# Layer 1's last row group normalised by GpSimd, and the query scales worked out in two parts

## The reference

```python
xn = _layernorm(x)                                 # (x - mean) / sqrt(var + 1e-5)
s = _L1_attn_ref(xn, L1_attn_W_qkv, L1_attn_W_out) # local attention in chunks of 64 rows, 16 heads of 8,
                                                   # plus a cross term with the mean keys of earlier chunks
# the gate, _L1_ffn_ref(xn, ...):
nx = xn * rsqrt(mean(xn * xn) + 1e-6) * g1         # _rmsnorm
Q = nx @ Wq.T ; Kc = nx @ Wkc.T ; Vc = nx @ Wvc.T  # 4 heads share keys and values, softmax over all rows
X = xn + attention(Q, Kc, Vc) @ Wo.T
g = silu(X + moe(_rmsnorm(X, g2)))
out = x + s * g
```

## Time and profile before

| what | value |
|---|---|
| time, median of 3 runs | 676.07 us (674.52 to 678.64) |
| the profiled execution's own time | 676.78 us |
| its span, first to last instruction | 674.6 us |
| granted TensorE clock, mean over the span | 0.966 |
| busy: PE / DVE / ACT / POOL | 609.1 / 484.8 / 353.0 / 356.0 us |
| the chunk stage's place in the span | about 212 to 305 us |

### The profile page before, as it was taken

One profiled execution on the slowest core, in us unless ns is written; L12 is line 12 of the kernel. 1 busy time (PEld: TensorE's weight loads), 2 busy tenths in 40 slices (PEclk: granted clock), 3 DMA queues, 4 the chain that ended last, 5 costly groups with the idle time before them and its releaser, 6 DMA issues.

```text
span 674.6 us, 12623 instructions
## 1 busy us (share of the span) xinstructions
PE 609.1 (90%) x4528; PEld 409.6 (61%) x4529; DVE 484.8 (72%) x1140; ACT 353.0 (52%) x714; POOL 356.0 (53%) x369
## 2 busy tenths in 40 slices
PE   4885889967998889896999999999999998999996
PEld 2564789944775556554555555555545553688885
DVE  5764345422987778769877788888888883788986
ACT  2643355421675445462667676777666666433231
POOL 6507400064463545170688887888787778524311
PEclk9989799988999899998999999999999998899999
DMA  9701012120000000000000000000000000000101
GB/s 290 321 1 48 31 48 63 47 55 24 1 0 2 1 2 3 2 3 1 0 1 1 1 0 2 1 1 1 0 1 1 1 0 1 1 1 1 32 1 32
DMA packets 16616, 17.33 MB, mean 26 GB/s; under 512 B 1712, under 2 KB 15024, under 8 KB 16176
## 3 DMA queue, kind: packets, MB, share of 16 engines
q1 hardware_dynamic: 15536, 14.49, 6.5%
q0 software_dynamic: 1024, 2.10, 1.0%
HBM read 11.34 MB, written 5.24 MB: 25 GB/s over the span
## 4 chain that ended last, share of the span: by engine, by line
PE 72%; DVE 14%; ACT 5%; issue 4%; another core or an unknown queue 2%; DMA 2%; POOL 1%; SPq 0%; DVEq 0%; ACTq 0%
PE ps L2052 13%; PE ps L2042 10%; PE ps L2032 8%; PE ps L2180 5%; PE ps L1764 4%; PE ps L1747 3%; DVE region L1086 3%; PE ps L1855 3%; PE ps L2170 2%; PE ps L2172 2%; PE ps L2171 2%; PE ps L1845 2%; DVE region L1067 1%; PE ps L1756 1%
## 5 line engine op out<-in xcount | busy, mean ns | idle before, releaser
L1086 DVE TENSOR_REDUCE region<-ps 128x1 f32<-128x512 f32 x256 | 160.7, 683 | 38.6 <-PE ps L2032 38.1
L1537 ACT ACTIVATE region<-ps 128x512 f32<-128x512 f32 x256 | 138.2, 600 | 60.3 <-PE ps L2042 60.3
L767 POOL TENSOR_TENSOR region<-region 128x512 f32<-128x512 f32 x80 | 109.0, 1365 | 42.5 <-ACT region L1537 38.5
L2042 PE MATMUL ps<-qmr,kr 98*128 98x512 f32 x256 | 111.8, 441 | 2.6 <-ACT region L1537 1.8
L2032 PE MATMUL ps<-kr,qmr 96*128 96x512 f32 x256 | 102.8, 411 | 2.1 <-DVE region L1086 1.3
L2052 PE MATMUL ps<-region 128*32 128x512 f32 x512 | 94.5, 616 | 0.0
L2059 PE MATMUL ps<-region,ones 128*32 128x512 f32 x192 | 94.3, 614 | 0.0
L772 POOL TENSOR_TENSOR region<-region 128x512 f32<-128x512 f32 x64 | 82.1, 1282 | 11.9 <-ACT region L1537 8.1
L2042 PEld LDWEIGHTS ps<-qmr,kr 98*128 98x128 f32 x256 | 48.7, 191 | 54.7 <-issue 28.9
L2032 PEld LDWEIGHTS ps<-kr,qmr 96*128 96x128 f32 x256 | 49.1, 193 | 15.6 <-DVE region L1086 9.0
L1764 PE MATMUL ps<-region 128*128 128x128 f32 x272 | 40.8, 298 | 19.1 <-ACT region L1384 12.9
(11 more groups left out here) (283 smaller groups left out, 1209.8 us busy)
## 6 DMA issues: line engine op xcount, KB each, us to landing
region<-in_w SPq DMA_DIRECT2D x2, 2048.0 KB, 12.9
slots_in<-zeros SPq DMA_DIRECT2D x1, 1536.0 KB, 9.4
region<-slots_in SPq DMA_DIRECT2D x6, 256.0 KB, 2.8
slots_out<-og SPq DMA_DIRECT2D x6, 256.0 KB, 2.4
e<-in_e SPq DMA_DIRECT2D x1, 1152.0 KB, 15.3
x<-in_x SPq DMA_DIRECT2D x4, 256.0 KB, 3.6
out<-y SPq DMA_DIRECT2D x3, 256.0 KB, 2.3
e<-in_e SPq DMA_DIRECT2D x1, 576.0 KB, 16.2
```

The lines of the kernel that those rows point to most:

```text
L767: ins = pool.tensor_tensor(o, held(tiles[0]), held(tiles[1]), ALU.add)
L1086: dve.tensor_reduce(mxp[:, u // HM, u % HM:u % HM + 1], bank(b), AX.X, ALU.max).then_inc(mx_read, 1)
L1537: act.activation(pm[:, t // 2, t % 2 * HM * P:(t % 2 + 1) * HM * P], bank(SCORE_BANKS[n % 3]), ACT.Exp, scale=SCM).then_inc(p_whole, 1)
L2042: pe.matmul(bank(SCORE_BANKS[n % 3]), kr[0:M_ROWS, t * P:(t + 1) * P], qr[0:M_ROWS, parity, :], start=True, stop=True).then_inc(st_filled, 1)
```

## The change

The four normalisations of row group 3 leave ScalarE's queue, where they stood between tile 2's exponentials and the first `qkv` drain, and are written by GpSimd, right behind the group's inverse deviation. TensorE's transposes of that group wait on GpSimd's counter. The query scales of groups 0 to 2 are computed by four instructions of 12 columns ahead of `expand` of group 1; those of group 3 by four instructions of 4 columns behind the normalisation. The `qkv` drains of tiles 12 to 15 wait for the second part, the others for the first.

```diff
         beside = {0: [("turn1", 1)], 1: [("k1", 1), ("q1", 1), ("expand", 1), ("gated", 3)],
-                  2: [("v1", 1), ("turn1", 2), ("xn1", 3)],
+                  2: [("v1", 1), ("turn1", 2)],
...
+            def second_roots(groups):
+
+                r = slice(TG * groups[0], TG * (groups[-1] + 1))
+                pool.wait_ge(rstd_ready[3], groups[-1] + 1)
+                link(pool.tensor_tensor(msq[:, r], mv[:, r, 1], rstd[:, r], ALU.mult))
+                link(pool.tensor_tensor(msq[:, r], msq[:, r], rstd[:, r], ALU.mult))
+                link(pool.tensor_scalar(msq[:, r], msq[:, r], 1e-6, None, ALU.add))
+                pool.tensor_tensor(rstdq[:, r], msq[:, r], mhalf[:, r], ALU.pow).then_inc(rstdq_ready, 1)
+
             def rows_normalised(g):

                 inverse_deviation(3, g, 1e-5)
-
-                pool.wait_ge(rstd_ready[3], NG)
-                link(pool.tensor_tensor(msq[:, :], mv[:, :, 1], rstd[:, :], ALU.mult))
-                link(pool.tensor_tensor(msq[:, :], msq[:, :], rstd[:, :], ALU.mult))
-                link(pool.tensor_scalar(msq[:, :], msq[:, :], 1e-6, None, ALU.add))
-                pool.tensor_tensor(rstdq[:, :], msq[:, :], mhalf[:, :], ALU.pow).then_inc(rstdq_ready, 1)
+                normalised(g)
+                second_roots((g,))
                 pool.wait_ge(x1_ready, NG)
                 link(pool.memset(ka[:, :, R_ROWS:M_ROWS], 1.0))

+            second_roots((0, 1, 2))
...
             def projected1(u):
                 W3 = D + 2 * DM
-                act.wait_ge(rstdq_ready, 1)
+                act.wait_ge(rstdq_ready, 1 if 2 * u + 1 < TG * (NG - 1) else 2)
...
                 for t in range(TG):
-                    if g > 0:
+                    if g == NG - 1:
+                        pe.wait_ge(xn0_ready, TG + t + 1)
+                    elif g > 0:
                         pe.wait_ge(xn_ready, NT + TG * (g - 1) + t + 1)
                     ins = pe.transpose(o[:, P * t:P * (t + 1)], xn[:, TG * g + t, :], ident[:, :])
```

## The result

| kernel | median, us | runs | ratio to before, 95% interval |
|---|---|---|---|
| before | 675.92 | 6 | |
| changed | 670.58 | 6 | 0.993 (0.9903 to 0.9957) |
| before, in a later comparison | 671.89 | 26 | |
| changed, in the later comparison | 668.35 | 10 | 0.9947 (0.992 to 0.9974) |

The change makes the kernel faster by 0.5 to 0.7%, 5.3 us in the first comparison and 3.5 us in the second, where the forecast had 3.4. Both intervals contain the forecast 3.4 us, which is a ratio of 0.995.

The account below looks back on a forecast made before the run. Bound: TensorE's chain, stalled by group 3's tiles late in ScalarE's queue. Saving 1.84 us of stall plus 1.58 of clock, 3.4 us, gave 673.4 from the profiled 676.78 and 672.7 from the median; forecast 673.1, range 670.8 to 676.8.

Parts of the forecast that it names:

- What bounds: Group 3's normalisations wait in ScalarE's queue behind tile 2's exponentials, leaving TensorE idle 2.09 us before its transposes.
- Part 1: Query scales of groups 0 to 2 fit GpSimd's wait before `expand`: 12-column power 2.30 us, delay kept at 0.06 us.
- Part 2: Group 3's normalisation on GpSimd at 0.446 us per tile: last transpose at 227.35 instead of 229.19, saving 1.84 us.
- Part 4: TensorE's clock stays high behind group 3's transposes, since its idle time shrinks to about 0.5 us: saves 1.58 us.
- first rival: The clock behind group 3's transposes falls all the same, so only 1.84 us is saved: 674.9 us, chance 0.22.
- Part 5: Group 3's query scales on GpSimd behind the tiles take 2.0 us, to 229.3, well before they are needed: no cost.
- the slack: Spare time behind the earlier transposes: 2.3 us for tile 2's exponentials, 1.1 us for VectorE's passes over tile 3's scores.
- The sum: Whole kernel: 1.84 us of stall plus 1.58 of clock, 3.4 us off; 673.4 for the profiled execution, forecast 673.1.
- Slower tiles: Group 3's four tiles take GpSimd 3.13 us, the stall saves 0.49 us: taken as 675.8 us, chance 0.08.
- mutual hindrance of GpSimd and VectorE: All four tiles of group 3 cost 1.397 us each, last transpose 1.9 us later: 678.7 us, chance 0.05.
- The low stretch at 284 goes too: The low-clock stretch from 284.0 to 287.4 us also disappears, another 1.6 us off: 671.5 us, chance 0.10.

Follow-up runs that it names:

- the scales alone: The changed kernel with group 3's normalisation, and TensorE's waits for it, left on ScalarE: 674.9 us against 674.34 before, ratio 1.0001.
- the tiles twice: The changed kernel with GpSimd computing each tile of group 3 twice, once into an unread buffer: 671.58 us, ratio to before 0.9985.
- the normalisation alone: The changed kernel with the query scales of all 16 tiles in one piece behind GpSimd's tiles: 670.65 us, ratio to before 0.9962.
- the order on ScalarE: The kernel before, with ScalarE's four normalisations of group 3 moved ahead of tile 2's exponentials: 670.75 us, ratio 0.9949.
- the clock alone: The kernel before, with 14 overwritten transposes filling TensorE's idle time ahead of group 3's transposes: 673.71 us against 674.34, ratio 1.0.
- three-and-one kernel: The changed kernel with group 3's last tile normalised by ScalarE: 666.55 us, ratio to before 0.9925; on a further chip 647.14 us, ratio 0.9925.

## Why the prediction was right, point by point

- **What bounds.** Right. The time at which the last tile of group 3 is there set the chain. Taking only ScalarE's order out of the way gave 2.93 of 3.39 us; making GpSimd about as late as ScalarE gave all of it back but 0.09.
- **Part 1, the early scales.** The 12-column power was forecast at 2.30 us and took 2.30; the delay of `expand`, kept at 0.06, was none. Alone it was worth nothing that could be seen, as the prediction's sum, which gives it no gain, had it.
- **Part 2, the tiles.** 0.446 us forecast, 442 to 449 ns measured. From the shift's start to the last transpose it was 229.19 − 225.16 = 4.03 us and is 228.33 − 226.19 = 2.14: 1.89 saved, 1.84 forecast. The rule of the Trainium skill (GPSIMD Engine Reference, § 8 Key points) that VectorE is about twice as fast as GpSimd in elementwise work decided nothing here, and no run here compares these two engines: the one to be compared was ScalarE, with some 390 ns per tile against 446, and what counted was when each could start.
- **Part 4, the clock.** 1.58 forecast; the rest of 3.39 − 1.89 = 1.50 measured, and 1.48 when only the gap was filled. Of the profiles whose last transpose came as late as before, with the gap left unfilled (before, the scales alone, the tiles twice), all three fell to the low level right behind it; of the nine whose stall was shortened or filled none did. One argument for it was weaker than the prediction took it. It leaned on the wait of 1.52 us before 214.92, behind which the clock "stayed at 1.00", but its row ends 1.1 us behind that wait, while by its own reading the low level comes some 3.3 us after the idle begins. The trace does have 1.00 up to 229.2 us. Yet behind the same wait the low level comes in one of the twelve profiles, that of the normalisation alone (shown there). Nor does a gap of 1.8 us decide it: three of ten profiles fell behind the one before the last keys. That a shortened wait keeps the clock is therefore likely and not certain, which is what the prediction's first rival allowed for.
- **Part 5 and the slack.** Right: the second part of the scales delays nobody. That the first drain does not wait for its scales rests on the split, which the prediction called harmless and did not price as needed: it is worth 0.7 us.
- **The sum.** 3.4 forecast for the profiled execution; 3.39 where the programs differ, 3.5 in the second comparison. The forecast of 673.1 was 2.5 us above the first median. The step that was mis-sized is the bottom of the range, "671.5 less some spread is 670.8". It let one low stretch near 284 go. The profile on which the sum was made held two more that the changed kernel's lacks, worth 2.5 us at 567 and 574 us besides the 1.36 near 284, and those two come and go in one and the same kernel. That six runs of each kernel differ by 5.3 us and later ones by 3.5 lies within the interval of the first comparison (2.9 to 6.6 us).
- **The rivals.** Slower tiles and mutual hindrance of GpSimd and VectorE did not come, as the rows had it; made on purpose, the price was as computed. "The low stretch at 284 goes too" came in both profiles of the changed kernel; whether through the change is open. A short stall alone doesn't do it: the order on ScalarE and the clock alone kept the stretch. The scales alone lack it in their profile, and yet their 12 runs show the kernel before's time (ratio 1.0001) and clock (0.9699 against 0.9697), which speaks against a lasting effect of the change there.

## What to carry to other kernels

Where an engine is idle, look for when its input could have been there, not for who makes it: here the data waited 2 us in another engine's queue behind work with slack, and reordering that queue alone recovers most. Price a short TensorE stall together with the clock behind it, which in the profiles here cost nearly as much as the stall, and call that part likely, not certain. When an effect is under 1%, measure the length between two fixed instructions around it; for the changed kernel it was 8.48 us in both profiles, while whole times moved by four to six.

## What the runs showed of the hardware that was not expected

- TensorE's clock fell to the 1.2 GHz level behind a stall in which it still did a transpose every 0.77 to 0.87 us, with waits of only 0.47 to 0.54 us before each (the one profile of the tiles-twice kernel, 0.56 behind it). Behind transposes every 0.34 to 0.44 us, in both profiles of the change, it stayed at 1.00.
- Waits of equal length were followed by either level: 1.52 us before a group's keys by the low one in one of twelve profiles, 1.82 us before the last keys' transposes in three of ten.
- GpSimd's power costs 1.04, 2.30 and 2.93 us for 4, 12 and 16 columns of 128 partitions: a straight line of 0.1575 us per column.
- The same kernel took 675.9, 674.3, 671.9 and 651.0 us by medians in the four comparisons, of which the last three ran on three different chips. In the last one's profile of the three-and-one kernel the shift of group 3 stands at 202.3 us instead of 221.5 to 227.4. The chains of the kernel before and of both profiles of the changed one hold a wait of 9.2 to 11.9 us near 150 us that is put down to "another core or an unknown queue"; the chain of this one holds none there. What it is, no run here shows; compare kernels only within one chip.
